# Layer 1 of a two-layer graph-attention kernel: a gather ring of six rounds in place of five, paid for with smaller and shared buffers

## The chip, the cores and the metric

One NeuronCore of a Trainium2 chip runs the whole program. The metric is the device time of one execution in microseconds (us), and less is better. The engines are PE (TensorE, matrix products), DVE (VectorE), ACT (ScalarE), POOL (GpSimd, which here issues the gathers) and SP (SyncE, which here issues the plain transfers). The core's 16 DMA engines move what POOL and SP have issued.

## The reference

Two layers of graph attention over 3125 nodes and 50000 edges, each with a layer norm and a relu ahead of it and a residual sum behind it. The change touches the second (layer 1) alone. For a node s with outgoing edges to nodes d:

```python
h = jnp.maximum(_layernorm(x, axis=-1), 0.0)          # x: what layer 0 left, 3125 x 1024
h = h @ W                                             # 1024 x 1024
al, ar = h @ a_l, h @ a_r
e = jnp.exp(-jax.nn.leaky_relu(al[src] + ar[dst], negative_slope=0.1))
rowsum = jax.ops.segment_sum(e, src, num_segments=N)
h_prime = jax.ops.segment_sum(e[:, None] * h[dst], src, num_segments=N)
x = x + jax.nn.elu(h_prime / (rowsum[:, None] + 1e-5))
```

## The kernel before

Layer 0 runs first and leaves two tables in HBM: layer1_rows (one row of 1028 floats for each node: the normed features, and behind them the node's score ar) and x1 (the residual). The sum over edges is taken ahead of the product with W, so layer 1 gathers rows of features, sums them with weights, and multiplies the sums by W once for each tile.

The function collect does layer 1. Its 3125 source nodes form 25 tiles (t) of 128; a tile has 4 windows of 32 nodes. The edges of a window fill up to four rounds (c = 0 to 3) of 128 edges, and a fifth round (c = 4, "last") is shared by pairs of windows. POOL gathers a round with one indirect DMA for each window: 128 rows of 4112 bytes, one edge on each partition. That makes 4 gathers for each of the rounds 0 to 3 and 2 for the last one, 18 in a tile and 441 in all. The rounds 0 to 3 of all tiles go in turn into the slots of the buffer ring1, of which there are RING; the last rounds have a buffer of their own, ring1_last, of two slots. POOL waits ahead of a round's first gather until PE has used what lay in that slot, which is the own round RING places earlier; used_before works out the count that ring_free must have reached, and it is the only thing that POOL waits for.

DVE and ACT then make the round's weights, two rounds ahead of PE (AHEAD = 2): DVE adds the scores (into weight, line L1800), takes the leaky slope (into steep, L1803), masks places that belong to another node with the table other (L1805), and ACT takes the exponential (L1665). PE adds the round into the PSUM tensor acc (L1717: 16 matmul records for a round, 8 for the last) and signals ring_free. DVE's add has to wait for the round's gathers.

Behind a tile's five rounds PE sums the weights (L1727), ACT divides (mean, L1671), PE turns the mean (L1736, two halves), ACT and DVE split it into a high and a low float32r part, and PE multiplies by W1 in three products for each of 8 chunks (L1750 to L1752, 48 matmuls). These pieces are dealt out by hand between the rounds of the next two tiles (the function steps): in the order of PE a round c = 0 is followed by 18 products, c = 1 by 12, c = 2 and c = 3 by half of the turns each, and the last round by the sums and 18 products.

The end of a tile is finish: ACT makes exp(min(h, 0)) in the buffer below, DVE adds max(h, 0) to it (into y, L1825) and then x1 and minus one (from x1t, L1828), and SP stores y into the output (L1639), loads the next tile's x1 (L1634) and a row of scores for a later tile (neg_al, L1620). Each engine works through its own list of instructions in order, so one that waits holds up what stands behind it.

At the start of the stage SP also loads W1, 8 chunks of 512 KB, by landing buffers: below, y and x1t take turns (L1628). ACT rounds a chunk to its high part (L1696) and DVE takes the low part (L1842), one chunk with each of the first eight rounds; SP may load the next chunk into a landing buffer when DVE has split what lay there.

Of the kernel before, what the change touches and what calls it, by code (L numbers as in the profile page):

```python
# [7 lines left out]
BF16 = mybir.dt.bfloat16  # L8
# [3 lines left out]
ALU = mybir.AluOpType  # L12
# [3 lines left out]
P = 128  # L16
N = 3125
D = 1024
# [4 lines left out]
SLOPE1 = 0.1  # L23
LN_EPS = 1e-5
SUM_EPS = 1e-5
NEG = -1.0e30
# [22 lines left out]
NWP = TILES * QW  # L49
RC = 5  # L50
# [44 lines left out]
def rows(table, tile, size=P):  # L95
    return table[bass.ds(tile * P, size), :]
# [25 lines left out]
def build(nc, x, src, dst, w0, att_src, att_dst, bias, w1, a1, out):  # L122
    def dram(name, shape, dt=F32):
        return nc.dram_tensor(name, shape, dt, kind="Internal").ap()

    pack_d = dram("edge_pack", [PULL_ROWS, PULL], I32)
    last_d = dram("row_last_windows", [EPAD // PULL], BF16)
    win_d = dram("edge_windows", [1, EPAD], BF16)
    va_d = dram("w1_att", [2 * KC, P])
    list_d = dram("src_lists", [NWP * REGION, 1])  # L130
    table0 = dram("layer0_rows", [NP, ROW0])
    table1 = dram("layer1_rows", [NP, ROW])
    x1_d = dram("x1", [NP, D])
    al_d = dram("al_rows", [TILES, P])
    with ExitStack() as ctx:
        ident = ctx.enter_context(nc.sbuf_tensor("ident", [P, P], F32))
        flag = ctx.enter_context(nc.sbuf_tensor("flag", [1, 1], I32))
        with ExitStack() as sparse:
            def sb(name, shape, dt=F32):
                return sparse.enter_context(nc.sbuf_tensor(name, shape, dt))  # L140

            found = sb("found", [NWP, 2])
            found_last = sb("found_last", [P, 1])
            shift = sb("shift", [P, 1])
            iota = sb("iota", [P, PAIR])
            nid = sb("nid", [P, 1])
            with ExitStack() as layer0:
                def sb0(name, shape, dt=F32):
                    return layer0.enter_context(nc.sbuf_tensor(name, shape, dt))

                idx0 = sb0("idx0", [P, RC, NWP], U32)
                idx0_last = sb0("idx0_last", [P, PAIRS], U32)
                idx0_first = sb0("idx0_first", [P, OWN, 2 * QW], U32)
                idx0_last_first = sb0("idx0_last_first", [P, 2 * QP], U32)
                loc0 = sb0("loc0", [P, RC, NWP])
                loc0_last = sb0("loc0_last", [P, PAIRS])
                a_src = sb0("a_src", [P, TILES, H])
                a_dst = sb0("a_dst", [P, TILES, H])
                near16 = sb0("near16", [P, CAP], BF16)
                lists_and_project(nc, x, src, dst, w0, att_src, att_dst, w1, a1, pack_d, last_d, win_d, va_d,  # L160
                                  list_d, table0, ident, found, found_last, shift, idx0, idx0_last, idx0_first,
                                  idx0_last_first, loc0, loc0_last, a_src, a_dst, iota, nid, near16)
                attend(nc, x, bias, va_d, list_d, table0, table1, x1_d, al_d, ident,
                       idx0, idx0_last, idx0_first, idx0_last_first, loc0, loc0_last, a_src, a_dst, iota, nid,
                       near16)
            idx1 = sb("idx1", [P, RC, NWP], U32)
            idx1_first = sb("idx1_first", [P, RC, 2 * QW], U32)
            loc1 = sb("loc1", [P, RC, NWP])
            lists_by_src(nc, list_d, ident, found, found_last, shift, idx1, idx1_first, loc1, flag)
            collect(nc, w1, table1, x1_d, al_d, ident, idx1, idx1_first, loc1, iota, out)  # L170
        dense(nc, x, src, dst, w0, att_src, att_dst, bias, w1, a1, out, ident, flag)

# [1343 lines left out]


def collect(nc, w1, table1, x1_d, al_d, ident, idx1, idx1_first, loc1, iota, out):
    RING = 5
    LASTS = 2  # L1520
    AHEAD = 2
    EVEN = TAIL // 16 * 16
    with ExitStack() as ctx:
        ctx.enter_context(nc.cleanup_on_exit())

        def sb(name, shape, dt=F32):
            return ctx.enter_context(nc.sbuf_tensor(name, shape, dt))
# [6 lines left out]
        w_high = sb("w1_high", [P, KC, D], F32R)  # L1534
        w_low = sb("w1_low", [P, KC, D], F32R)
        neg_al = [sb(f"neg_al{k}", [P, P]) for k in range(2)]
        other = sb("other", [P, RC, P])
        weight = [sb(f"weight1_{k}", [P, RC, P]) for k in range(2)]
        steep = [sb(f"steep1_{k}", [P, P]) for k in range(2)]
        ones = sb("ones1", [P, 1])  # L1540
        total = sb("total", [P, 1])
        inv = sb("inv", [P, 1])
# [2 lines left out]
        hT_low = sb("hT1_low", [P, KC, P], F32R)  # L1545
        below = sb("below1", [P, D])
        y = sb("y1", [P, D])
        x1t = sb("x1t", [P, D])
        landing = [below, y, x1t]

        acc = [ctx.enter_context(nc.psum_tensor(f"acc1_{k}", [P, D], F32)) for k in range(2)]
        tp = ctx.enter_context(nc.psum_tensor("tp_l1", [P, HALF], F32))
# [12 lines left out]
        steepened = sem("steepened")  # L1565
# [49 lines left out]
        @block.sync  # L1615
        def _(sp):
            def load_al(t):
                if t >= 2:
                    sp.wait_ge(added, RC * (t - 1))
                sp.dma_start(neg_al[t % 2][:, :], al_d[t:t + 1, :].to_broadcast([P, P])).then_inc(al_in[t % 2], 16)  # L1620

            load_al(0)
            load_al(1)
            for c in range(KC):
                k = c % len(landing)
                if c >= len(landing):
                    sp.wait_ge(w_split, c - len(landing) + 1)
                sp.dma_start(landing[k][:, :], w1[c * P:(c + 1) * P, :]).then_inc(w_in[k], 16)  # L1628
            load_al(2)
            sp.wait_ge(w_split, KC)  # L1630
            for t in range(TILES):
                if t >= 1:
                    sp.wait_ge(y_done, t)
                sp.dma_start(x1t[:, :], rows(x1_d, t)).then_inc(x1_in, 16)  # L1634
                if t + 3 < TILES:
                    load_al(t + 3)
                sp.wait_ge(y_done, t + 1)
                if t < TILES - 1:
                    sp.dma_start(rows(out, t), y[:, :]).then_inc(y_out, 16)  # L1639
                else:  # L1640
                    sp.dma_start(out[t * P:t * P + EVEN, :], y[0:EVEN, :]).then_inc(y_out, 16)
                    sp.dma_start(out[t * P + EVEN:N, :], y[EVEN:TAIL, :]).then_inc(y_out, 16)
            sp.wait_ge(y_out, 16 * (TILES + 1))
# [17 lines left out]
        def _(act):  # L1661
# [18 lines left out]
            def finish(t):  # L1680
                act.wait_ge(projected, t + 1)
                if t >= 1:
                    act.wait_ge(above_done, t)
                act.activation(below[:, :], mm[:, :], ACT.Relu, scale=-1.0).then_inc(below_done, 1)
                act.wait_ge(below_done, t + 1)
                act.activation(below[:, :], below[:, :], ACT.Exp, scale=-1.0).then_inc(e_done, 1)
# [88 lines left out]
        def _(dve):  # L1775
# [14 lines left out]
            def weigh(r):  # L1790
                t, c = divmod(r, RC)
                if c == 0:
                    outside(t)
                    if t >= 2:
                        dve.wait_ge(total_done, t - 1)
                    dve.wait_ge(al_in[t % 2], 16 * (t // 2 + 1))
                dve.wait_ge(gathered[place(t, c)], landings[r])
                q, wide = (QW, WIN) if c < OWN else (QP, PAIR)
                to = weight[t % 2][:, c, :]
                then(dve.tensor_tensor(to.rearrange("p (q n) -> p q n", q=q),  # L1800
                                       neg_al[t % 2][:, :].rearrange("p (q n) -> p q n", q=q),
                                       fetched(t, c)[:, :, D:D + 1].to_broadcast([P, q, wide]), ALU.add), added)
                then(dve.scalar_tensor_tensor(out=steep[c % 2][:, :], in0=to, scalar=SLOPE1, in1=to,  # L1803
                                              op0=ALU.mult, op1=ALU.min), steepened)
                then(dve.scalar_tensor_tensor(out=to, in0=other[:, c, :], scalar=NEG, in1=steep[c % 2][:, :],  # L1805
                                              op0=ALU.mult, op1=ALU.add), masked)

            def invert(t):
                dve.wait_ge(total_done, t + 1)
# [10 lines left out]

            def finish(t):
                dve.wait_ge(e_done, t + 1)
                if t >= 1:
                    dve.wait_ge(y_out, 16 * t)
                then(dve.scalar_tensor_tensor(out=y[:, :], in0=mm[:, :], scalar=0.0, in1=below[:, :],  # L1825
                                              op0=ALU.max, op1=ALU.add), above_done)
                dve.wait_ge(x1_in, 16 * (t + 1))
                then(dve.scalar_tensor_tensor(out=y[:, :], in0=y[:, :], scalar=-1.0, in1=x1t[:, :],  # L1828
                                              op0=ALU.add, op1=ALU.add), y_done)

            dve.memset(ones[:, :], 1.0).then_inc(ones_set, 1)
# [1385 lines left out]
```

## Time and profile before

| | us |
|---|---|
| median of three runs | 2025.16 (2017.92 to 2032.6) |
| the profiled execution's own time | 2027.11 |
| its span, first to last instruction | 2025.0 |
| layer 1's first gather is issued | 1291.4 |
| its last gather is issued | 1957.2 |

The difference of 2.1 us between the profiled execution's time and its span lies outside the program. Layer 1 takes from 1290 us to the end, some 735 us; everything ahead of it is the same code before and after. Times in rows are microseconds from the span's start.

### The profile page before, as it was taken

To read this page: it belongs to the slowest core of one execution; us is meant where nothing else is said; L and a number is where in the kernel's file an instruction comes from. 1 tells how busy PE (TensorE), PEld (TensorE's weight loads), DVE (VectorE), ACT (ScalarE), POOL (GpSimd) and SP (SyncE) were. 2 spreads that over 40 slices of the span, in tenths; PEclk is the share of its full clock that TensorE was granted. 3 is DMA by queue.
4 is the path that set the end of the run, shared out by engine and by line. 5 is a ranking of instruction groups with operands and counts; after the bars stand their busy time and mean duration, and the time that the engine had idled before them with its cause. 6 is when DMAs were issued, how large, how long until landed. Compare 5 with 4: busy or idle time off the path is not lost. (4 is left out here: it accounts for less than half of the span.)

```text
span 2025.0 us, 27950 instructions
## 1 busy us (share of the span) xinstructions
PE 1583.1 (78%) x10493; PEld 837.8 (41%) x10493; DVE 1233.0 (61%) x2870; ACT 445.0 (22%) x768; POOL 1039.1 (51%) x1060
## 2 busy tenths in 40 slices
PE   3897999897168777777677676169999999999896
PEld 2444545443034344344344333014544544454454
DVE  4999999997147777777777877342333333333332
ACT  3332333221002221122211221021222221122121
POOL 1121212111656776767767650376666766666630
PEclk9897999998577787878878887569999999999898
DMA  7321333221889999999999983599999999999961
GB/s 234 93 93 57 87 93 96 85 94 48 348 304 347 381 362 382 369 374 381 379 376 373 380 330 113 206 410 352 365 360 359 352 363 355 344 370 349 330 213 47
DMA packets 170575, 554.44 MB, mean 274 GB/s; under 512 B 32195, under 2 KB 37178, under 8 KB 170080
## 3 DMA queue, kind: packets, MB, share of 16 engines
q0 software_dynamic: 128128, 417.93, 56.0%
q1 hardware_dynamic: 38708, 121.44, 17.4%
q10 hardware_dynamic: 3600, 13.24, 1.8%
q8 instruction: 85, 1.39, 0.3%
q14 instruction: 54, 0.44, 0.1%
HBM read 547.51 MB, written 53.52 MB: 297 GB/s over the span
## 5 line engine op out<-in xcount | busy, mean ns | idle before, releaser
L1064 POOL DMA_INDIRECT ring<-layer_rows,idx x360 | 394.4, 1096 | 188.3 <-issue 86.8
L1655 POOL DMA_INDIRECT ring<-layer_rows,idx x360 | 369.7, 1027 | 186.3 <-issue 94.8
L588 PE MATMUL mm<-w_sb,hT 128*128 128x512 f32 x800 | 362.6, 607 | 0.0
L1190 PE MATMUL acc<-ring,weight 128*32 128x256 f32 (+1 forms) x3600 | 334.6, 480 | 26.4 <-issue 14.3
L1717 PE MATMUL acc<-ring,weight 128*32 128x512 f32 x1600 | 221.3, 630 | 39.7 <-issue 34.5
L588 PEld LDWEIGHTS mm<-w_sb,hT 128*128 128x128 f32 x800 | 153.4, 197 | 174.7 <-issue 174.7
L1190 PEld LDWEIGHTS acc<-ring,weight 128*32 128x32 f32 (+1 forms) x3600 | 154.0, 137 | 155.3 <-issue 118.4
L1817 DVE TENSOR_TENSOR hT_low<-tp_l,hT_high 128x512 fp32r<-128x512 f32 x50 | 34.6, 692 | 300.3 <-issue 248.4
L467 POOL CAST row_l<-asd 128x4 bf16<-128x4 f32 x25 | 4.8, 190 | 336.9 <-DVE asd L677 336.9
L1750 PE MATMUL mm_l<-w_high,hT_high 128*128 128x512 f32 x400 | 169.1, 423 | 8.5 <-issue 6.0
L1752 PE MATMUL mm_l<-w_high,hT_low 128*128 128x512 f32 x400 | 163.4, 409 | 10.1 <-issue 10.0
L1751 PE MATMUL mm_l<-w_low,hT_high 128*128 128x512 f32 x400 | 162.4, 406 | 8.0 <-issue 8.0
L1128 PE MATMUL turned<-ident,ring 128*12 128x128 bf16 x450 | 34.9, 234 | 149.6 <-ACT score_T L1074 82.8
L1268 DVE TENSOR_REDUCE highest<-wide 128x4 f32<-128x512 f32 x125 | 85.1, 681 | 78.5 <-issue 28.6
L1717 PEld LDWEIGHTS acc<-ring,weight 128*32 128x32 f32 x1600 | 46.4, 112 | 154.2 <-issue 154.1
L773 DVE TENSOR_TENSOR_SCAN running<-mine,nought 100x1792 f16<-100x1792 f16 x28 | 108.8, 3886 | 1.0
L1750 PEld LDWEIGHTS mm_l<-w_high,hT_high 128*128 128x128 f32 x400 | 77.4, 194 | 68.9 <-issue 52.1
L1665 ACT ACTIVATE weight<-weight 128x128 f32<-128x128 f32 x125 | 38.7, 309 | 304.2 <-DVE weight L1805 155.2
L1074 ACT ACTIVATE score_T<-turned 128x128 bf16<-128x128 f32 (+1 forms) x125 | 33.5, 268 | 308.0 <-DMA s_i<-in_src_dram 167.7
L1322 DVE SCALAR_TENSOR_TENSOR own<-own,self_w,acc 128x256 f32<-128x256 f32 x100 | 48.1, 481 | 79.3 <-DMA own<-layer_rows 48.6
L1128 PEld LDWEIGHTS turned<-ident,ring 128*12 128x12 bf16 x450 | 14.8, 85 | 187.3 <-issue 134.1
L677 DVE CUSTOM_DVE_ANT_0 prod<-row_l,att_bc 128x256 f32<-128x256 f32 x200 | 84.8, 424 | 10.8 <-issue 2.8
(271 smaller groups left out, 2419.0 us busy)
## 6 DMA issues: line engine op xcount, KB each, us to landing
layer_rows<-row_l ACTq DMA_DIRECT2D x25, 517.0 KB
layer_rows<-row_l SPq DMA_DIRECT2D x25, 514.0 KB
own<-layer_rows SPq DMA_DIRECT2D x25, 512.0 KB
x<-xb SPq DMA_DIRECT2D x25, 512.0 KB
x1t<-x SPq DMA_DIRECT2D x25, 512.0 KB
xt<-in_x_dram SPq DMA_DIRECT2D x24, 512.0 KB
xb<-in_x_dram SPq DMA_DIRECT2D x24, 512.0 KB
out_dram<-y SPq DMA_DIRECT2D x24, 512.0 KB
```

The lines of the kernel that those rows point to most:

```text
L588: last = pe.matmul(mm[k][:, f * HALF:(f + 1) * HALF], hT[k][:, c, :], w_sb[:, c, f * HALF:(f + 1) * HALF], start=c == 0, stop=c == KC - 1)
L677: dve.tensor_tensor_reduce(out=prod[:, :], in0=row[k][:, h * C:(h + 1) * C], in1=att_bc[:, j, h * C:(h + 1) * C], scale=1.0, scalar=0.0, o ...
L773: then(dve.tensor_tensor_scan(running[:, :], mine[c % 2][:, :], nought[0:NWP, 0:1].to_broadcast([NWP, CW]), 0.0, ALU.add, ALU.max), scanned)
L1064: pool.indirect_dma_start(out=ring[:, t % 2, blocks(c), :][:, q, :], out_offset=None, in_=table0, in_offset=bass.IndirectOffsetOnAxis(ap=i ...
L1128: last = pe.matmul(turned[q * WIN:q * WIN + SCORES, 0:P], ring[:, t % 2, blocks(c), D + H:ROW0][:, q, :].bitcast(BF16), ident16[:, :], sta ...
L1190: last = pe.matmul(acc[t % 2][k * n:(k + 1) * n, h, :], by[:, k, h, :], ring[:, t % 2, blocks(c), h * C:(h + 1) * C][:, k, :], start=c == ...
L1268: then(dve.tensor_reduce(highest[:, c, :], wide[r % 2][:, :, :], AX_X, ALU.max), maxed)
L1655: pool.indirect_dma_start(out=fetched(t, c)[:, q, :], out_offset=None, in_=table1, in_offset=bass.IndirectOffsetOnAxis(ap=idx, axis=0), bo ...
L1717: last = pe.matmul(acc[t % 2][q * wide:(q + 1) * wide, f * HALF:(f + 1) * HALF], weight[t % 2][:, c, q * wide:(q + 1) * wide], fetched(t, ...
L1750: pe.matmul(mm[:, cols], hT_high[:, c, :], w_high[:, c, cols], start=c == 0, stop=False)
L1751: pe.matmul(mm[:, cols], hT_high[:, c, :], w_low[:, c, cols], start=False, stop=False)
L1752: last = pe.matmul(mm[:, cols], hT_low[:, c, :], w_high[:, c, cols], start=False, stop=c == KC - 1)
```

## The change

Four edits in collect, and one in the caller:

1. RING goes from 5 to 6: used_before now asks for the own round six places earlier. A slot takes 16.4 KB of each partition's on-chip memory; the other edits give up buffers.
2. x1t is gone. SP loads x1 into y, so it must wait until the store of the tile before has left y (y_out in place of y_done); DVE's first operation of finish writes into below instead of y, the second reads below and y and writes y. ACT's first write into below now waits for y_done instead of above_done.
3. W1 has two landing buffers, below and y, in place of three.
4. The two buffers steep are gone: the slope is taken in place in weight.
5. other (the mask) and loc1 (the places in a window, whole numbers under 128) are bf16 in place of float32.

```diff
--- before.py
+++ after.py
@@ -165,7 +165,7 @@
                        near16)
             idx1 = sb("idx1", [P, RC, NWP], U32)
             idx1_first = sb("idx1_first", [P, RC, 2 * QW], U32)
-            loc1 = sb("loc1", [P, RC, NWP])
+            loc1 = sb("loc1", [P, RC, NWP], BF16)
             lists_by_src(nc, list_d, ident, found, found_last, shift, idx1, idx1_first, loc1, flag)
             collect(nc, w1, table1, x1_d, al_d, ident, idx1, idx1_first, loc1, iota, out)
         dense(nc, x, src, dst, w0, att_src, att_dst, bias, w1, a1, out, ident, flag)
@@ -1516,7 +1516,7 @@
 
 
 def collect(nc, w1, table1, x1_d, al_d, ident, idx1, idx1_first, loc1, iota, out):
-    RING = 5
+    RING = 6
     LASTS = 2
     AHEAD = 2
     EVEN = TAIL // 16 * 16
@@ -1534,9 +1534,8 @@
         w_high = sb("w1_high", [P, KC, D], F32R)
         w_low = sb("w1_low", [P, KC, D], F32R)
         neg_al = [sb(f"neg_al{k}", [P, P]) for k in range(2)]
-        other = sb("other", [P, RC, P])
+        other = sb("other", [P, RC, P], BF16)
         weight = [sb(f"weight1_{k}", [P, RC, P]) for k in range(2)]
-        steep = [sb(f"steep1_{k}", [P, P]) for k in range(2)]
         ones = sb("ones1", [P, 1])
         total = sb("total", [P, 1])
         inv = sb("inv", [P, 1])
@@ -1545,8 +1544,7 @@
         hT_low = sb("hT1_low", [P, KC, P], F32R)
         below = sb("below1", [P, D])
         y = sb("y1", [P, D])
-        x1t = sb("x1t", [P, D])
-        landing = [below, y, x1t]
+        landing = [below, y]
 
         acc = [ctx.enter_context(nc.psum_tensor(f"acc1_{k}", [P, D], F32)) for k in range(2)]
         tp = ctx.enter_context(nc.psum_tensor("tp_l1", [P, HALF], F32))
@@ -1630,8 +1628,8 @@
             sp.wait_ge(w_split, KC)
             for t in range(TILES):
                 if t >= 1:
-                    sp.wait_ge(y_done, t)
-                sp.dma_start(x1t[:, :], rows(x1_d, t)).then_inc(x1_in, 16)
+                    sp.wait_ge(y_out, 16 * t)
+                sp.dma_start(y[:, :], rows(x1_d, t)).then_inc(x1_in, 16)
                 if t + 3 < TILES:
                     load_al(t + 3)
                 sp.wait_ge(y_done, t + 1)
@@ -1680,7 +1678,7 @@
             def finish(t):
                 act.wait_ge(projected, t + 1)
                 if t >= 1:
-                    act.wait_ge(above_done, t)
+                    act.wait_ge(y_done, t)
                 act.activation(below[:, :], mm[:, :], ACT.Relu, scale=-1.0).then_inc(below_done, 1)
                 act.wait_ge(below_done, t + 1)
                 act.activation(below[:, :], below[:, :], ACT.Exp, scale=-1.0).then_inc(e_done, 1)
@@ -1800,10 +1798,10 @@
                 then(dve.tensor_tensor(to.rearrange("p (q n) -> p q n", q=q),
                                        neg_al[t % 2][:, :].rearrange("p (q n) -> p q n", q=q),
                                        fetched(t, c)[:, :, D:D + 1].to_broadcast([P, q, wide]), ALU.add), added)
-                then(dve.scalar_tensor_tensor(out=steep[c % 2][:, :], in0=to, scalar=SLOPE1, in1=to,
-                                              op0=ALU.mult, op1=ALU.min), steepened)
-                then(dve.scalar_tensor_tensor(out=to, in0=other[:, c, :], scalar=NEG, in1=steep[c % 2][:, :],
-                                              op0=ALU.mult, op1=ALU.add), masked)
+                then(dve.scalar_tensor_tensor(out=to, in0=to, scalar=SLOPE1, in1=to, op0=ALU.mult, op1=ALU.min),
+                     steepened)
+                then(dve.scalar_tensor_tensor(out=to, in0=other[:, c, :], scalar=NEG, in1=to, op0=ALU.mult, op1=ALU.add),
+                     masked)
 
             def invert(t):
                 dve.wait_ge(total_done, t + 1)
@@ -1820,12 +1818,10 @@
 
             def finish(t):
                 dve.wait_ge(e_done, t + 1)
-                if t >= 1:
-                    dve.wait_ge(y_out, 16 * t)
-                then(dve.scalar_tensor_tensor(out=y[:, :], in0=mm[:, :], scalar=0.0, in1=below[:, :],
+                then(dve.scalar_tensor_tensor(out=below[:, :], in0=mm[:, :], scalar=0.0, in1=below[:, :],
                                               op0=ALU.max, op1=ALU.add), above_done)
                 dve.wait_ge(x1_in, 16 * (t + 1))
-                then(dve.scalar_tensor_tensor(out=y[:, :], in0=y[:, :], scalar=-1.0, in1=x1t[:, :],
+                then(dve.scalar_tensor_tensor(out=y[:, :], in0=below[:, :], scalar=-1.0, in1=y[:, :],
                                               op0=ALU.add, op1=ALU.add), y_done)
 
             dve.memset(ones[:, :], 1.0).then_inc(ones_set, 1)
```

The order of instructions stays the same on every engine; what moves is which buffer is written and what is waited for. On SP, the start of the stage and its first two turns of the loop, before (names in brackets are semaphores, under the name that the program's first stage gave to the same number: p_mean_done is w_split, p_part_done is y_done, p_rest_done is added):

```order
L1628 DMA x1t<-in_L_gnn_W_dram 128x1024
L1628 DMA below<-in_L_gnn_W_dram 128x1024 [waits p_mean_done]
L1628 DMA y<-in_L_gnn_W_dram 128x1024 [waits p_mean_done]
...
L1634 DMA x1t<-x 128x1024 [waits p_mean_done]
L1620 DMA neg_al<-al_rows 128x128 [waits p_rest_done]
L1639 DMA out_dram<-y 128x1024 [waits p_part_done]
L1634 DMA x1t<-x 128x1024 [waits p_part_done]
```

And after (p_eps_set is now w_split, p_parts_ready is y_out):

```order
L1626 DMA y<-in_L_gnn_W_dram 128x1024
L1626 DMA below<-in_L_gnn_W_dram 128x1024 [waits p_eps_set]
L1626 DMA y<-in_L_gnn_W_dram 128x1024 [waits p_eps_set]
...
L1632 DMA y<-x 128x1024 [waits p_eps_set]
L1618 DMA neg_al<-al_rows 128x128 [waits p_rest_done]
L1637 DMA out_dram<-y 128x1024 [waits p_part_done]
L1632 DMA y<-x 128x1024 [waits p_parts_ready]
```

The third chunk of W1 now waits for a split, and the load of x1 waits for the store just issued to land, with the load of neg_al behind it. On DVE, one round's mask, the end of a tile and the next tile's start, before (p_last_in is e_done, p_win_done is x1_in, p_parts_ready here is y_out):

```order
L1803 SCALAR_TENSOR_TENSOR steep_0<-weight_0 128x128 [waits p_rest_done]
L1805 SCALAR_TENSOR_TENSOR weight_0<-other,steep_0 128x128 [waits p_row_out0]
L1817 TENSOR_TENSOR hT_low<-tp_l,hT_high 128x512 [waits p_pack_done,p_row_out1]
L1825 SCALAR_TENSOR_TENSOR y<-mm_l,below 128x1024 [waits p_parts_ready,p_last_in]
L1828 SCALAR_TENSOR_TENSOR y<-y,x1t 128x1024 [waits p_win_out,p_win_done]
L1779 TENSOR_TENSOR other<-iota,loc 128x512 [waits p_part_done]
```

And after:

```order
L1801 SCALAR_TENSOR_TENSOR weight_0<-weight_0 128x128 [waits p_rest_done]
L1803 SCALAR_TENSOR_TENSOR weight_0<-other,weight_0 128x128 [waits p_row_out0]
L1815 TENSOR_TENSOR hT_low<-tp_l,hT_high 128x512 [waits p_pack_done,p_row_out1]
L1821 SCALAR_TENSOR_TENSOR below<-mm_l,below 128x1024 [waits p_last_in]
L1824 SCALAR_TENSOR_TENSOR y<-below,y 128x1024 [waits p_win_out,p_win_done]
L1777 TENSOR_TENSOR other<-iota,loc 128x512 [waits p_part_done]
```

The count and the place of DVE's operations are the same; the wait for the store moved from DVE to SP. POOL's list of gathers is the same too, with smaller counts to wait for.

## Rows read from the trace of the kernel before

**Rows 1.** The page's first line.

```profile
span 2025.0 us, 27950 instructions
```

**Rows 2.** Stretches: length; PE, PEld, DVE, ACT, POOL busy; PE clock, DMA share, GB/s.

```profile
1300.00:1370.00 70.00, 40.12 (x184) 12.54 (x185) 23.58 (x54) 13.37 (x23) 50.77 (x50) 0.70 1.03 411
1400.00:1900.00 500.00, 464.61 (x2582) 246.25 (x2582) 171.58 (x425) 103.45 (x186) 343.01 (x333) 0.98 0.97 354
...
1960.00:1984.00 24.00, 24.00 (x144) 13.49 (x144) 9.91 (x25) 5.98 (x11) 0.00 (x0) 1.00 0.14 48
...
600.00:1100.00 500.00, 369.99 (x3672) 201.38 (x3671) 375.66 (x901) 101.92 (x196) 353.01 (x319) 0.80 1.01 371
```

**Rows 3.** Groups by line: POOL, 1400 to 1980 us (busy, mean ns, idle, releasers).

```profile
L1655 POOL DMA_INDIRECT ring<-layer_rows,idx x324 | 332.8, 1027 | 171.4 <-issue 84.8 <-remote 45.0 <-PE acc L1717 41.6
```

**Rows 4.** What POOL waited for, 1400 to 1957 us (us, times, longest).

```profile
POOL ring L1655 <- remote: 45.0, 24, 2.3
POOL ring L1655 <- PE acc L1717: 41.6, 22, 5.8
```

**Rows 5.** What PE waited for, 1400 to 1980 us (us in total, times, longest).

```profile
PE tp_l L1736 <- issue: 12.3, 7, 2.4
PE mm_l L1752 <- issue: 7.9, 13, 1.0
```

**Rows 6.** PE in order of time: rounds, turns and sums of three tiles.

```profile
1605.71 1.94 PE L1717 MATMUL acc<-ring_last,weight 128*64 128x512 f32 x8
...
1619.37 1.92 PE L1717 MATMUL acc<-ring,weight 128*32 128x512 f32 x16
...
1629.11 1.94 PE L1717 MATMUL acc<-ring_last,weight 128*64 128x512 f32 x8
1630.97 1.28 PE L1727 MATMUL sums<-ones,weight 128*128 128x1 f32 x10
1636.50 3.63 PE L1717 MATMUL acc<-ring,weight 128*32 128x512 f32 x15
...
1659.03 1.94 PE L1717 MATMUL acc<-ring_last,weight 128*64 128x512 f32 x8
```

**Rows 7.** POOL in order of time: two waits of the same tiles, and a plain step.

```profile
1613.79 0.99 POOL L1655 DMA_INDIRECT ring<-layer_rows,idx  x1 [0.30 <-issue]
1615.09 0.99 POOL L1655 DMA_INDIRECT ring<-layer_rows,idx  x1 [0.31 <-issue]
...
1624.59 0.99 POOL L1655 DMA_INDIRECT ring<-layer_rows,idx  x1 [2.03 <-remote]
```

**Rows 8.** DVE in order of time: the total and the weights of 1639 to 1644 us.

```profile
1639.16 0.16 DVE L1812 TENSOR_SCALAR total<-sums 128x1 f32<-128x1 f32 x1 [2.87 <-DMA s_i<-in_src_dram]
...
1643.63 0.29 DVE L1800 TENSOR_TENSOR weight<-neg_al,ring 128x128 f32<-128x128 f32 x1 [3.13 <-DMA ring<-layer_rows,idx]
```

**Rows 9.** All engines in order of time, 1310 to 1333 us.

```profile
1310.95 1.10 POOL L1655 DMA_INDIRECT ring<-layer_rows,idx_first  x1 [0.30 <-issue]
...
1319.26 0.33 SPq L1628 DMA_DIRECT2D below<-in_L_gnn_W_dram  x1
...
1320.72 0.29 DVE L1800 TENSOR_TENSOR weight<-neg_al,ring 128x128 f32<-128x128 f32 x1 [1.49 <-DMA ring<-layer_rows,idx_first]
...
1325.38 1.04 ACT L1696 ACTIVATE w_high<-x1t 128x1024 fp32r<-128x1024 f32 x1
```

**Rows 10.** DVE and SP in order of time: ends of tiles.

```profile
1607.51 1.23 DVE L1828 SCALAR_TENSOR_TENSOR y<-y,x1t 128x1024 f32<-128x1024 f32 x1
...
1608.76 0.34 SPq L1639 DMA_DIRECT2D out_dram<-y  x1
...
1630.66 1.22 DVE L1828 SCALAR_TENSOR_TENSOR y<-y,x1t 128x1024 f32<-128x1024 f32 x1
```

**Rows 11.** What POOL waited for in layer 0, 600 to 1100 us.

```profile
POOL ring L1064 <- PE acc L1190: 35.5, 32, 2.4
POOL ring L1064 <- remote: 33.2, 31, 1.5
```

## The prediction

> **What bounds the kernel now.** The page gives the span, 2025.0 us [rows 1]; its shares of it mix two layers, so I read the stretches next [rows 2]. In layer 1's steady part, 1400 to 1900 us, PE is busy 464.6 of 500 us at a granted clock of 0.98, which is the upper of its two levels nearly throughout; POOL 343.0, DVE 171.6, ACT 103.5. The DMA engines are 0.97 busy but move 354 GB/s, against 411 in 1300 to 1370. So PE and the gathers run close together, and the other engines have room.
>
> Per tile. A tile has 138 matmul records (64 and 8 of rounds, 10 of sums, 8 of turns, 48 of products). 2582 records in 500 us are 18.7 tiles, 26.7 us each [rows 2]. PE in order of time shows that this mean is made of two kinds: from one last round to the next it takes 1629.11 - 1605.71 = 23.4 us, and then 1659.03 - 1629.11 = 29.9 [rows 6]. 23.4 is what PE needs when nothing is in its way: after the last gather, 1960 to 1984, it is busy 24.00 of 24 us [rows 2]. In the long tile a round of 16 matmuls that takes 1.92 us elsewhere has 15 of them spread over 3.63 [rows 6]. PE thus loses 3.3 us a tile.
>
> POOL. A gather takes 1.03 us and 0.30 to the next, 1.33, so 18 take 23.9 us [rows 3, 7]. POOL too could go faster than 26.7. It stands idle for 45.0 + 41.6 = 86.6 us in 46 waits, less the usual 0.30 each 72.8 us [rows 4]. Since ring_free is the only thing it waits for, the label "remote" is the same wait, where the profile found no matmul that ended just then.
>
> What PE waits for is the view on which my forecast turns [rows 5]. The longest sums are "issue", 12.3 and 7.9 us in 580; no gather, and no weight that waited for one, is among the large ones. DVE does wait for gathers [rows 8], but it works two rounds ahead of PE, so this reaches nobody.
>
> What, then, do POOL's waits show? The gather at 1624.59 stood 1.7 us longer than usual [rows 7]. It belongs to the third round of its tile, and with five slots it needs the tile before's second round, which PE shows from 1619.37 to 1621.29 [rows 6]: over 3 us earlier. And DVE takes the total at 1639.16 after a wait of 2.87 us, though the sums are shown to end at 1632.25 [rows 6, 8]. PE's signals reach the others 3 to 7 us after the ends that are shown, at times when the transfers are heavy. The Trainium skill (Perfetto Trace Analysis, "Summary: the profiler window per engine type") says that a matmul's end in a profile is estimated and that the signal's way is hidden. By that rule the trace agrees, but it gives no size for it. POOL's waits, in short, follow from PE's late signals and PE's own losses.
>
> **The change, part by part.**
>
> Ring of six. The gathers' bytes and number stay. In 1300 to 1370 the transfers are already at 411 GB/s, the highest of any stretch, so asking earlier brings nothing there: 0. In the steady part POOL, with a further slot, skips its first waits, and is one round (4 x 1.33 = 5.3 us) further ahead after about two tiles of 2.8 us gain each. Then the ring is full again, and it goes at PE's pace. PE does not wait for gathers, so its 26.7 us stay: 0. The bounds are wide. From below: if PE's losses go, the slower of PE and POOL sets the pace, 23.9; (26.7 - 23.9) x 22 tiles = -62 us. From above: if the heavier transfers cost PE one more such loss of 3.3 us in each pair of tiles, 11 x 3.3 = +36. I take 0 because layer 0 is the nearest row: it has a ring of ten rounds, and POOL still waits 63 times for PE in 600 to 1100 us, 68.7 us in all [rows 11], at 371 GB/s [rows 2]. A ring of twice the depth did not remove such waits; it fills up too.
>
> The end. POOL's last gather is out up to 5.3 us earlier, and in that time PE runs at 23.4 and not at 26.7 us a tile: 5.3 x (1 - 23.4 / 26.7) = -0.7 us.
>
> W1 by two buffers. The third chunk used to be loaded at the start. Now its load is issued at 1319.26 and ACT wants it at 1325.38 [rows 9], 6.1 us later. For the time of half a megabyte in this stretch the nearest row is the gather that ended its issue at 1312.05 and was used at 1320.72 [rows 9], 8.7 us at most. So ACT may be held 0 to 2.6 us, once; later chunks have two rounds, about 10 us. What hides it is the saturated DMA: PE is fed by gathers there and busy only 40 of 70 us [rows 2], and a chunk less ahead of the gathers gives them its time. I take 0; without that cover it is +2.6.
>
> x1 into y. SP waits for the store to land before the load of x1. Each is 512 KB; by the same 8.7 us the two take 17.4, plus 0.8 of issue, 18.2 us from 1608.76, and DVE wants x1 at 1630.66 [rows 10], 21.9 later. It is hidden by 3.7 us in the short tiles and by more in the long ones. The load of neg_al behind it on SP is for three tiles on. If the cover were gone, DVE would stand, and behind it the weights of the next tile's rounds. The wait for the store leaves DVE: nothing, since it was long over. Store and load no longer come at once, which evens the transfers a little; it is in the lower bound above.
>
> Slope in place and bf16. The order of DVE's operations stays. If the bf16 mask took half or twice its time, the two operations for other, under 1 us a tile together (by their size, next to the 1.2 us of a full 128x1024 [rows 10]), would change by less than that, and DVE is idle two thirds of the time [rows 2]: 0.
>
> The sum against the profiled execution: 2027.1 - 0.7 = 2026.4. The median of the runs lies 2.0 us under the profiled one, so 2024.
>
> **Rivals.**
>
> R0, PE keeps its pace, as above: 2024, its own range 2008 to 2038.
>
> R1, the losses go. For it: POOL's waits are short and many, each just behind a late signal; with six slots POOL asks for a round 5.3 us older, whose signal has long come, the gathers flow evenly, and x1 and the store no longer fall together. If PE's long tiles then shrink to the pace of POOL, 2027 - 62 = 1965; by half, 1996. Against: PE shows no wait for gathers.
>
> R2, slower. The long tiles are those in which POOL has issued without a stop since 1624.59. If PE's loss comes from transfers at full rate, a sixth slot lets POOL run a round longer into it, PE loses 3.3 us more in each pair of tiles, and the time is 2027 + 36 = 2063. It decides as soon as the rate stays over some 400 GB/s for longer than now; at 411 GB/s, in 1300 to 1370, PE is at its worst, but there it also waits for its first gathers [rows 2]. The Trainium skill (SBUF — State Buffer, "Who interferes with whom") says that a DMA never contends with a compute engine. By that rule R2 would be nothing and the time 2024 or less; the late totals speak against it being the whole story, and so R2 keeps its chance.
>
> R3, the DMA engines are the limit. By bytes, 354 GB/s x 26.7 us = 9.45 MB a tile; at 411 GB/s this takes 23.0 us, so by the rows it is not. The time would be 2026. The Trainium skill (DMA: Bandwidth & Descriptors, "Where 436 GB/s comes from") puts the limit between HBM and on-chip memory at some 358 GB/s, which would make 354 the ceiling; the 411 of an earlier stretch speaks against it.
>
> **How the numbers follow.** A measurement of this kernel tells about 1% from no change, 20 us. R0 0.36 and R3 0.05 end within it. R1 has 0.37, of which 0.03 for a gain too small to be told. R2 has 0.22, 0.02 of it for the wait for x1 running out. So faster 0.34, same 0.44, slower 0.22. The predicted time is R0's, 2024. The range takes in R0 and R3, most of R1 down to 1975 and R2's price: 1975 to 2063.
>
> **What the profile after would show.** R0: the steady part still at 354 GB/s and 26.7 us a tile, POOL's waits still some 70 us, with the first of them later. R1: the long tiles gone, over 370 GB/s, POOL nearly without waits. R2: more than every second tile of 29.9 us or longer. W1: ACT standing ahead of the third chunk's copy by at most 2.6 us. x1: no wait of DVE ahead of the second operation of finish. I would be wrong if PE's loss were in truth due to POOL's stops and not the other way about.

## The result and the profile after

The changed kernel takes 2061.95 us (median of 4 runs, 2055.12 to 2074.54), the kernel before beside it 2028.88 (2017.92 to 2032.85): 1.0179 times as long, interval 1.0108 to 1.025. Timed again later, with 10 runs, it was 1.0102 times (1.0071 to 1.0133). So it is slower, by 1 to 2%. The profiled execution has a span of 2053.3 us, against 2025.0.

The stretches after, with the columns of [rows 2]:

```profile
600.00:1100.00 500.00, 360.45 (x3636) 195.31 (x3635) 372.86 (x889) 100.34 (x195) 351.84 (x316) 0.81 1.00 368
1300.00:1370.00 70.00, 34.56 (x150) 8.78 (x150) 20.37 (x44) 12.38 (x20) 52.40 (x51) 0.65 1.03 410
1500.00:1600.00 100.00, 87.67 (x483) 44.98 (x482) 31.67 (x73) 19.40 (x33) 62.15 (x63) 0.95 0.92 323
1700.00:1800.00 100.00, 89.74 (x476) 45.18 (x475) 31.75 (x73) 19.40 (x33) 60.65 (x62) 0.90 0.91 315
```

From 1700 to 1800 us PE has 476 records, 29.0 us a tile at 138 each; the mean of the fourth to the 21st tile is 28.25 us, 26.83 before. No tile of these takes 23.4 us any more (the shortest is 24.8). The transfers have become thinner, not heavier: 315 to 323 GB/s in these two stretches, against 354 before [rows 2]. What PE and POOL waited for from 1400 to 1980 us (us in total, times, longest), where [rows 4, 5] stood:

```profile
PE tp_l L1734 <- issue: 21.8, 5, 4.5
PE mm_l L1750 <- issue: 13.3, 20, 1.7
PE mm_l L1749 <- issue: 12.5, 17, 1.7
...
POOL ring L1653 <- PE acc L1715: 90.2, 32, 6.2
POOL ring L1653 <- remote: 24.3, 17, 1.9
```

POOL stands longer, 114.5 us in 49 waits. PE stands longer too, 58.5 us over all lines of this view where it was 38.3, and about half of that (29.7 us) lies within a run of products, where nothing in the code makes it wait. Three-microsecond windows through one tile show it best (columns of [rows 2]):

```profile
1506.00:1509.00 3.00, 3.00 (x19) 1.21 (x15) 1.84 (x2) 1.06 (x2) 2.39 (x3) 1.00 0.77 255
...
1512.00:1515.00 3.00, 1.66 (x6) 0.98 (x6) 0.78 (x2) 0.60 (x1) 2.10 (x3) 1.00 0.96 348
1515.00:1518.00 3.00, 0.79 (x2) 0.45 (x3) 0.70 (x3) 0.31 (x1) 1.97 (x2) 1.00 0.97 392
1518.00:1521.00 3.00, 2.27 (x14) 0.69 (x17) 1.48 (x6) 0.28 (x2) 0.00 (x0) 0.86 1.02 418
1521.00:1524.00 3.00, 3.00 (x13) 1.39 (x6) 1.48 (x6) 1.55 (x4) 1.01 (x2) 0.57 0.91 359
```

PE is busy 0.79 of 3 us from 1515 to 1518 and comes back in the window in which POOL is at rest (0.00). The granted clock falls only afterwards (0.86, then 0.57), so it is an effect of the stop, but one that costs too: the round that PE runs at 1519.44 takes 2.97 us in place of 1.92. POOL in order of time, then ACT and DVE, in the same tile:

```profile
1499.32 0.99 POOL L1653 DMA_INDIRECT ring<-layer_rows,idx  x1 [1.42 <-PE acc L1715]
...
1516.28 0.99 POOL L1653 DMA_INDIRECT ring<-layer_rows,idx  x1 [0.30 <-issue]
1522.69 0.99 POOL L1653 DMA_INDIRECT ring<-layer_rows,idx  x1 [5.42 <-PE acc L1715]
```

```profile
1513.52 0.60 ACT L1675 ACTIVATE hT_high<-tp_l 128x512 fp32r<-128x512 f32 x1 [1.55 <-remote]
1519.35 0.16 DVE L1810 TENSOR_SCALAR total<-sums 128x1 f32<-128x1 f32 x1 [3.59 <-DMA s_i<-in_src_dram]
```

POOL gathers without a stop from 1499.32 to 1517.27. PE's sums are shown to end at 1509.97, and DVE, which has stood waiting for them since 1515.76, gets them at 1519.35: 9.4 us later, and 2.1 us after POOL stopped. A late signal does not always wait for a stop, though: the turn that ends at 1506.90 reaches ACT at 1513.52, 6.6 us late, amid the gathers. I noted such late signals in the prediction and did not ask what held them up. That is the question for the runs.

### The profile page after: what moved, and what is told of

It is laid out like the page before. It is cut to its first block and busy times, and to the rows that moved or that the text cites. A ratio compares the mean times of both kernels' runs of the same rounds, so it can differ in the third digit from the quotient of the medians.

```text
span 2053.3 us, 27926 instructions
## 1 busy us (share of the span) xinstructions
PE 1585.4 (77%) x10493; PEld 835.9 (41%) x10493; DVE 1234.2 (60%) x2870; ACT 443.7 (22%) x768; POOL 1035.0 (50%) x1060
## 5 line engine op out<-in xcount | busy, mean ns | idle before, releaser
L1190 PE MATMUL acc<-ring,weight 128*32 128x256 f32 (+1 forms) x3600 | 327.8, 473 | 35.7 <-DVE weight L1303 26.7
L1675 ACT ACTIVATE hT_high<-tp_l 128x512 fp32r<-128x512 f32 x50 | 29.7, 594 | 325.7 <-PE tp_l L1734 203.7
L1750 PEld LDWEIGHTS mm_l<-w_high,hT_low 128*128 128x128 f32 x400 | 76.6, 192 | 36.2 <-issue 19.2
```

Of the source, the lines that this page charges most:

```text
L1190: last = pe.matmul(acc[t % 2][k * n:(k + 1) * n, h, :], by[:, k, h, :], ring[:, t % 2, blocks(c), h * C:(h + 1) * C][:, k, :], start=c == ...
L1750: last = pe.matmul(mm[:, cols], hT_low[:, c, :], w_high[:, c, cols], start=False, stop=c == KC - 1)
```

## The experiments

The runs were made in five groups, each on one chip with the kernel before timed beside them. That kernel took 2029.63 us in the first group, 1913.28 in the second, 2022.14 in the third, 1910.35 in the fourth and 1912.52 in the fifth. These are two kinds of place: I call them slow (2022 to 2030) and quick (1910 to 1913), as the forecasts of the later runs do by their times. The second and third groups name the same chip number, so it need not be the chip alone. A ratio is always to the kernel before in the same group.

### Which edit it is (first group, slow)

Ring of five with all the other edits (`RING = 6` to `RING = 5` in the changed kernel):

> The changed kernel with a ring of five rounds again; all its other edits stay (x1 loaded into y once the store has landed, slopes in place, places in bf16, W1 by two buffers). Theory A: PE loses time when POOL issues some 12 or more gathers without a stop, and the sixth slot makes these stretches follow one another in every tile; then nearly all of the 33 us is the ring's, and this takes 2020 to 2035 us. Theory B: the load of x1, which now waits for the store and so falls into the first rounds of the tile, moves the heavy time; then this takes 2050 to 2065. If both have a share it lies between.

Measured 1.0012 (0.9981 to 1.0043). With a ring of five the other edits together cost nothing that can be told.

x1 after the store, in the kernel before:

```diff
-                    sp.wait_ge(y_done, t)
+                    sp.wait_ge(y_out, 16 * t)
```

> The kernel before, ring of five, with one edit: SP waits for the store to have landed before it loads x1 (into its own buffer, as before). Theory A: no change, 2020 to 2035 us. Theory B: 2050 to 2065, with PE's loss in each tile and not in each second one.

Measured 1.0032 (1.0009 to 1.0055). Theory B falls.

Six rounds, and seven, without the other edits (in `collect` of the kernel before; `w_low` by one chunk):

```diff
-    RING = 5
+    RING = 6
```

> The kernel before with a ring of six rounds and none of the other edits. To have room for it only one chunk of the low part of W1 is kept, so the products with the low part all use that chunk (the same number and size of instructions; the output is not the reference's). Theory A: 2050 to 2070 us, over 27.5 us a tile in the steady part and PE's loss in every tile. Theory B: 2020 to 2035.

> As the kernel with six rounds and none of the other edits, one chunk of W1's low part kept, but with a ring of seven rounds. Theory A: POOL's unbroken stretches can grow by four more gathers, so 2055 to 2100 us, not less than with six. Theory B: 2020 to 2035. If depth only shifts where in a tile POOL stops, seven may be better than six again, near 2030: that would say that the depth itself is not the cause but how the stops fall in the tile's period.

Measured 1.0105 (1.0062 to 1.0147) with six and 1.0037 (1.0014 to 1.0061) with seven. So the sixth slot alone is slower; but seven is less slow than six, which theory A did not have. In its profiled execution, the lowest of its ten (2025.62 us), the ring with seven settles into one pattern: every tile from the fourth to the 21st takes 27.1 to 27.4 us. What PE waited for there, 1400 to 1900 us, and one tile's first turn with what follows it on ACT and what POOL does:

```profile
PE tp_l L1736 <- issue: 41.9, 17, 3.5
```

```profile
1520.18 0.66 PE L1736 MATMUL tp_l<-ident,mean 128*128 128x128 f32 x4
...
1525.42 0.63 PE L1736 MATMUL tp_l<-ident,mean 128*128 128x128 f32 x4 [2.08 <-issue]
```

```profile
1523.89 0.60 ACT L1677 ACTIVATE hT_high<-tp_l 128x512 fp32r<-128x512 f32 x1 [14.58 <-DMA edge_pack<-tail_pack]
```

```profile
1521.10 0.99 POOL L1655 DMA_INDIRECT ring<-layer_rows,idx  x1 [0.30 <-issue]
1524.07 0.98 POOL L1655 DMA_INDIRECT ring<-layer_rows,idx  x1 [1.98 <-PE acc L1717]
```

The first turn ends at 1520.84. ACT, idle for 14.58 us, gets its signal at 1523.89, 3.05 us later, 1.8 us after POOL stopped at 1522.09. Behind ACT come DVE's low part and then PE's second turn, which waits. The second turn waits in 17 of the some 18 tiles. The releaser that the row names (edge_pack) belongs to another part of the program: the label is what the profile found at that moment, no cause.

### Bytes, speed of POOL, kind of transfer (second group, quick)

x1 in its own buffer again, ring of six (`sp.wait_ge(y_done, t)`, `x1t` loaded):

> The changed kernel with a buffer of its own for x1 again, loaded beside the store, and one chunk only of W1's low part kept to make room for it (same instructions, output not the reference's). Ring of six, slopes in place, places in bf16, two buffers for W1. The ring of six alone measured 1.0105 times before, the whole change 1.0179. If x1's wait adds to the ring's price, this takes 2045 to 2055 us (1.008 to 1.013); if the difference between the two was only the spread of the runs, this is as slow as the changed kernel, 2055 to 2065.

Measured 0.9995 (0.9984 to 1.0007) at 1912 us. No verdict on x1, but the larger finding: in this place a ring of six costs nothing. Its stretch from 1400 to 1850 us, and those of the kernels before (slow) and after (slow):

```profile
1400.00:1850.00 450.00, 447.78 (x2636) 247.92 (x2635) 180.52 (x443) 106.29 (x192) 336.16 (x335) 1.00 1.02 402
```

```profile
1400.00:1850.00 450.00, 417.06 (x2329) 220.57 (x2329) 155.95 (x382) 94.15 (x167) 308.70 (x300) 0.98 0.97 355
```

```profile
1400.00:1850.00 450.00, 401.04 (x2183) 208.85 (x2181) 146.03 (x363) 86.87 (x157) 287.46 (x285) 0.95 0.94 337
```

In the quick place PE runs at its own 23.4 to 23.5 us a tile beside 402 GB/s, and POOL stops once in this stretch. Full transfers do not hold PE up as such. By the records (138 a tile), PE is idle 1.9 us a tile in the kernel before and 3.1 after, and busy 24.7 and 25.4: of the 1.8 us a tile that the change costs in these rows, two thirds are standing still, and one third is longer busy time, at a granted clock of 0.95 in place of 0.98.

A small operation of POOL ahead of each round:

```diff
+                if r:
+                    pool.memset(pause[:, :], 0.0).then_inc(paused, 1)
+                    pool.wait_ge(paused, r)
```

> The changed kernel with a small operation of POOL ahead of each round of gathers, for whose end POOL waits: some 0.3 to 0.5 us more per round, so a tile's 18 gathers take about 26 us in place of 23.9. Theory C: PE loses time when the transfers run at over some 390 GB/s for several us, which they do after POOL was let run ahead; paced, POOL asks for less at once, the losses shrink and the time falls to 2015 to 2040 us although POOL issues more slowly. Theory D: PE's loss comes from something in PE's own stream or from the number of slots, not from how fast POOL issues: 2055 to 2070.

Measured 1.0047 (1.003 to 1.0063), quick place: the pauses only cost. It tells nothing of theories C and D, since there is no loss there to cure.

Plain loads for gathers, and gathers of half rows:

```diff
-                    pool.indirect_dma_start(
-                        out=fetched(t, c)[:, q, :], out_offset=None, in_=table1, ...
+                    pool.dma_start(out=fetched(t, c)[:, q, :], in_=table1[first:first + P, :])
```

> The changed kernel with each gather replaced by a plain load of 128 consecutive rows of the same table, same bytes (the output is not the reference's): POOL no longer writes a descriptor for each row. Theory C (the rate of the transfers): the DMA engines are as full as before or fuller, PE still loses time where the rate is near 400 GB/s; 27 us a tile or more, 2040 us or over. Theory E (POOL's descriptor writing holds up PE's signals): with it gone PE runs without losses at 23.4 us a tile if the data come in time, about 1990 us, and PE's signals come at once even at full rate.

> The changed kernel with gathers of half rows: the same number of gathers and of row descriptors, half the bytes, products of rounds read the half that is there (the output is not the reference's). Theory C: transfers stay well under 300 GB/s, PE runs at 23.4 us a tile or at POOL's pace of 23.9, layer 1's steady part takes 24 us a tile, about 1960 to 1980 us. Theory E: POOL issues as much as before, so PE's losses and late signals stay: 27 to 28 us a tile, 2040 us or over.

One run each: 1958.07 us and 1904.42, beside 1913.28. Both had to be had again in a slow place. The forecast's "same bytes" for the plain loads is not so: the traces have some 2300 packets of 4112 bytes a tile with plain loads and some 2040 with gathers, so a tile moves 10.6 MB in place of 9.5.

### The same in a slow place (third group)

> The changed kernel once more, timed beside the kernel before. On a chip where the kernel before takes some 2030 us, it repeats 1.018 (2055 to 2070 us); on a chip where the kernel before takes 1913 us, on which the ring of six with a buffer of its own for x1 measured 0.9995, x1's wait can cost a little: 1.000 to 1.004, 1910 to 1922 us. So the sign of the change would hang on the chip.

Measured 1.0102 (1.0071 to 1.0133), slow place.

> The kernel with gathers of half rows again, on the chip that this call gets. On a chip like the first (before at 2030 us): theory C, heavy transfers hold PE up, gives 23.4 to 24 us a tile, 1955 to 1980 us; theory E, POOL's descriptor writing, gives 26.7 us a tile or more, 2030 us or over. On a chip like the second it repeats 1904 us.

2047.33 us, beside 2022.14 (one run; the changed kernel's ten lie between 2032.89 and 2051.91).

> The kernel with plain loads in place of gathers again. On a chip like the first: theory C gives 28 us a tile or more, 2060 us or over, since all bytes and more are there; theory E gives a clear gain against the gathers, some 25 to 26 us a tile as on the second chip. On a chip like the second it repeats 1958 us.

1992.08 us (one run), 34 us more than in the quick place, all of it ahead of layer 1's steady part: from the first tile's last round to the 25th's it takes 625.4 us here and 627.0 there. With gathers of half rows the same distance is 677.8 us here and 575.4 there.

The change without the products with W1's low part (the line of `pe.matmul` with `w_low` taken out):

> The changed kernel without the 16 products a tile with W1's low part (the output is not the reference's): PE needs some 19.6 us a tile, POOL 23.9. On a chip like the first, theory C: PE's losses of 4 us a tile come with the transfers' rate and fit into its idle time now, so 24 to 26 us a tile, 1970 to 2010 us, with PE still slow in places. Theory F (PE at full load is what makes packets stall): no long packets and no losses, 23.9 us a tile, DMA at 400 GB/s, about 1960. On a chip like the second: POOL's 23.9 us a tile, 1910 to 1925 us, the same as with the products.

2034.46 us (one run), though PE had a sixth less to do; a tile still takes 27.6 us. Half rows, then plain loads, 1400 to 1850 us:

```profile
1400.00:1850.00 450.00, 405.72 (x2228) 217.05 (x2229) 152.18 (x376) 89.88 (x162) 298.71 (x293) 0.95 0.65 193
```

```profile
1400.00:1850.00 450.00, 417.12 (x2399) 230.69 (x2399) 166.04 (x402) 96.83 (x176) 164.25 (x314) 0.98 1.03 410
```

This is the pair that decides. At 193 GB/s with gathers a tile takes 27.7 us; at 410 GB/s without gathers, 25.9, which is the time of 10.6 MB at that rate. PE's waits there are ordinary ones, for data and the weights made of them:

```profile
PE tp_l L1733 <- DVE hT_low L1814: 29.2, 16, 1.9
PE acc L1714 <- ACT weight L1662: 5.9, 14, 0.8
```

The trace also keeps the time at which a semaphore was raised. I compared those for PE's rounds, sums and turns with the ends of their last matmuls, 1400 to 1880 us. The next event of the semaphore comes over 1 us after the end in 91 of 144 cases in the kernel before, 72 of 134 in the changed one and 76 of 138 with half rows; in 0 of 150 with plain loads in the same place, and 0 of 160 with a ring of six and gathers in the quick place. Some of the late ones are only events that the trace lacks; where each event is given to one matmul alone, 56, 49 and 55 are left. Of the 28 late sums and turns of the changed kernel, 17 were raised in POOL's stops, which are 92 of the 480 us, 1.3 to 2.0 us after the last gather; 11 were raised while POOL gathered. (Rounds say little here, since a stop of POOL ends with a round's signal by its own wait.) No event of DVE or ACT in the changed kernel's trace is late, but it has only 330 of their 556; with plain loads, and in the quick place, it has them all.

Theory C falls, and theory F too. Theory E is half borne out, with a condition that it did not have: PE's signals come late where POOL gathers in a slow place, and not with plain loads there. Plain loads differ from gathers in more than the work of writing a descriptor for each row, though. Their rows are consecutive and not scattered, and POOL is idle for 304 of the 480 us. No run tells these apart, so which part of gathering holds the signals up is not shown. Nor is it shown that the late signals are what makes six slots slower than five: they are no more frequent after the change (72 of 134) than before it (91 of 144).

### Moving POOL's stops (fourth and fifth groups, quick)

POOL waits for the turn too, in the ring of six and in that of five:

```diff
                     pool.wait_ge(ring_free, used_before(t, c))
+                if c < OWN:
+                    u, k = divmod(OWN * t + c - RING, OWN)
+                    if k >= 2 and u >= 1:
+                        pool.wait_ge(turned_done, 2 * (u - 1) + k - 1)
```

> The changed kernel (ring of six), where POOL, ahead of the rounds whose slot was freed by the third or the fourth round of a tile, also waits for PE's turn that follows that round. The runs so far: where POOL gathers, PE's signals arrive up to 10 us late and mostly 1.2 to 2 us after POOL stops; with plain loads none is late. Theory E (POOL's gathers hold PE's signals up, and the sixth slot lets POOL run on while a signal is due): POOL now stands still just when the turn's signal is due, so the second turn's wait of up to 5 us goes, and on a chip where the kernel before takes some 2025 us this takes 1990 to 2040 us, less than the changed kernel's 2042 to 2062. If the signals are late for another reason, the further wait only delays the gathers: 2055 us or over. On a chip where before takes 1913 us: no difference, 1910 to 1925.

> The kernel before (ring of five) with the same further wait of POOL for the turns. Theory E: 1985 to 2025 us, at or under the kernel before. If the signals are late for another reason: 2035 us or over. On a chip where before takes 1913 us: within 0.5% of it.

> The kernel before with a ring of four rounds, nothing else. Theory E: POOL stops more often and is less far ahead when PE's signals are due; so the stretches of 14 gathers without a stop go and the time stays at that of before or falls, 2000 to 2035 us; the ring's depth would be of no use on such a chip. Theory R (the gathers' data come too late with four rounds): 2040 us or over, with PE waiting for weights that waited for data. On a chip where before takes 1913 us the ring of four loses its lead over the transfers: 1915 to 1960.

> The changed kernel with one pause of POOL of some 1.9 us a tile, ahead of the tile's first round, made of five small operations waited for one by one. POOL then needs 25.6 us a tile. Theory E: signals pass in that pause, which also splits the stretches of gathers; 26 to 27.5 us a tile, 2010 to 2045 us where before takes 2025. If only POOL's speed counts: 28 us a tile or more, 2060 us or over.

Measured, at 1910 us: 0.9991 (0.9972 to 1.001), 0.9997 (0.998 to 1.0013), 1.0036 (1.0016 to 1.0056) for the ring of four, and 1929.03 us in one run with the pause. So in a quick place four rounds are 0.4% short and five are enough. POOL ahead of a gather with the further wait, ring of six, has no stop (0.30 is the usual distance):

```profile
1509.95 0.99 POOL L1657 DMA_INDIRECT ring<-layer_rows,idx  x1 [0.30 <-PE tp_l L1738]
```

The same two kernels once more, for a slow place:

> The ring of six with POOL's further wait for the turns once more, for a chip on which the kernel before takes some 2025 us (the last call had one with 1910, where signals are never late). There, theory E: 0.985 to 1.007 times before, under the changed kernel's 1.010 to 1.018. If the signals are late for another reason than POOL's gathers: 1.015 or over. On a chip of 1910 us: 0.999 again.

> The ring of five with the same further wait once more. On a chip where before takes some 2025 us, theory E: 0.98 to 1.0 times before; if the signals are late for another reason: 1.005 or over. On a chip of 1910 us: 1.000 again.

It was a quick one: 1.0002 (0.9985 to 1.002) and 1.0001 (0.9988 to 1.0014). Whether stops put where signals are due cure the loss was therefore never tried in a slow place, and no version here is shown to beat the kernel before.

## Why the prediction was wrong

The forecast was no change, 2024 us, and the kernel is 1 to 2% slower. The step that failed is in "Ring of six": "PE does not wait for gathers, so its 26.7 us stay: 0". Its first half holds, before and after. What does not follow is the second. In a slow place PE and its readers depend on POOL in another way than through data: where POOL gathers, PE's signals come late, and PE itself stands more and at a lower clock with six slots, 28.25 us a tile in place of 26.83. A likely way, argued and not shown: when POOL may run on for another four gathers, its stops, in which over half of the late sums and turns are raised, fall elsewhere in the tile. The row of the nearest case that I chose, layer 0 with its ring of ten [rows 11], showed that the ring fills up. It could not show what a filling ring costs PE.

"POOL's waits, in short, follow from PE's late signals and PE's own losses" was half of a circle, and my last sentence named the other half ("if PE's loss were in truth due to POOL's stops and not the other way about") without giving it a chance. What the runs show is that the late signals and PE's stops amid products both go when plain loads take the place of the gathers.

R2 gave 2063 us, and the first measurement is 2062: right in sign and, by luck, in size. Its mechanism, transfers at full rate, was wrong. After the change the rate is lower, and with half the bytes the loss stays. I had put an association in place of a cause: PE was slow where the rate was high, in the two rows compared. The Trainium skill (SBUF — State Buffer, "Who interferes with whom") says that a DMA never contends with a compute engine; 402 GB/s beside a full PE in the quick place agrees, and plain loads at 410 GB/s in the slow place, with no late signal, agree too. The late signals with half rows in the slow place, 76 of 138 at 193 GB/s, are a hold-up beside gathers that the sentence does not tell of. The prediction gave a chance to the contrary on the strength of the late totals. These were real, but the gathers' and not the bytes'.

R1, the losses go: no. R3, the transfers as the limit: not in a slow place, where plain loads move 410 GB/s and the kernel before 355. In a quick place gathers move 402 to 408, PE has its 23.4 us, and the two limits all but coincide.

Term by term. The sixth slot: taken at 0, bounds -62 to +36; measured alone +21 us (1.0105). The pair of limits held it. W1 by two buffers: taken at 0, at most +2.6; ACT waited once, 0.53 us:

```profile
1325.54 1.06 ACT L1694 ACTIVATE w_high<-below 128x1024 fp32r<-128x1024 f32 x1 [0.53 <-DMA below<-in_L_gnn_W_dram]
```

x1 into y: "hidden by 3.7 us" held, for DVE has no wait ahead of the second operation of finish, and SP issues the load of x1 6.1 us after the store (18.2 us had been the bound for the two together):

```profile
1509.67 0.34 SPq L1637 DMA_DIRECT2D out_dram<-y  x1
1515.78 0.32 SPq L1632 DMA_DIRECT2D y<-x  x1
```

Slopes in place and bf16: taken at 0, and the mask, mean 691 ns before, takes 701:

```profile
L1777 DVE TENSOR_TENSOR other<-iota,loc 128x512 bf16<-128x512 f32 x17 | 11.9, 701 | 0.6
```

The sum of these, 1.0012 with a ring of five, was right. What stays open: what makes a place slow; by which way a gather holds up a signal; whether PE's stops amid products are the same hold-up felt by PE itself, as their end with POOL's stop suggests; whether the writing of the trace, which lacks events only where signals are late, has a part in it; and why five, six and seven rounds give 1.00, 1.01 and 1.004. The tiles suggest that it is which signal falls into a run of gathers (PE's products with six, the first turn with seven), but that is argued, not shown. Whether x1's wait adds to the ring's price (1.0105 against 1.0179 and 1.0102) is within the intervals.

## What to carry to other kernels

Before a queue is made deeper, ask not only who waits for its data but what else its producer does while it runs on: here, in a slow place, letting POOL run on for one round more cost 1 to 2% and gave nothing. When signals arrive later than the work that raises them is shown to end, look for what is going on in that time and ends just before they arrive, and give that a chance of its own. And measure a gain or loss of 1% in more than one place: this one exists in one kind and not in the other.

## What the runs showed of the hardware

The same kernel took 2012 to 2041 us in some groups and 1906 to 1918 in others. In layer 0 the rate differed already (368 to 375 against 385 to 388 GB/s, 600 to 1100 us).

Single packets of 4112 bytes, 0.16 us each as a rule, took up to 2.2 us. The time beyond 0.16 us, of packets over 0.25, comes to 43 us for each of the 16 engines in 500 us of layer 1 of the kernel before. With plain loads in the same place it is 0.8 us, with the ring of six in the quick place 1.6. But long packets are not the sign of late signals: with gathers of half rows they come to 70 us in either place, and in the quick one none of 161 signals is late.

A small operation of POOL between gathers cost under 0.1 us (0.11 busy, 0.27 in place of 0.30 to the next gather).
